# State-space layers unrolled, with the next layer's weight split and row normalisation beside the last chunk, decay sums of the first chunk ahead of the others, and the fourth stage's bias added tile by tile

## What is computed

```python
def _mamba2(u, in_w, conv_w, conv_b, dt_bias, A_log, Dp, rms_w, out_w):
    zxbcdt = u @ in_w.T                       # z, x, B, C, dt
    dt = softplus(dt + dt_bias)
    xBC = silu(causal_conv4(xBC) + conv_b)
    state = exp(dt * A) * state + (dt * x) B^T;  y = C . state + D * x
    y = y * silu(z)
    y = y * rsqrt(mean(y * y) + EPS) * rms_w
    return y @ out_w.T
h = x
for i in range(2):                            # N_LAYERS
    res = h
    h = layernorm(h) * ln_w[i] + ln_b[i]
    h = _mamba2(h, ...) + res
# fourth stage: t = t + (scan(...) * silu(z)) @ out_proj_w.T + out_proj_b
```

## Time and profile before

| | us |
|---|---|
| median of 3 runs | 1520.24 (1516.73 to 1520.94) |
| the profiled execution | 1520.59 |
| its span | 1518.6 |
| first layer opens, up to the first chunk's first exp | 100 to 171.7 |
| first layer's chunks | 171.7 to 380.8 |
| between the layers, up to the next first exp | 380.8 to 454.6 |
| second layer's chunks | 454.6 to 662.2 |
| end of the stage | 662.2 to 680.3 |
| fourth stage's opening | 744 to 788 |

### The profile page before, as it was taken

How to read it: one execution, slowest core, us unless ns; L and a number is a source line. 1 busy time by engine, 2 the same in 40 slices (tenths; PEclk the granted TensorE clock), 3 DMA queues, 4 the chain that set the end, 5 groups by cost and what they waited for, 6 DMA issues and landing times.

```text
span 1518.6 us, 33907 instructions
## 1 busy us (share of the span) xinstructions
PE 1245.3 (82%) x12366; PEld 857.0 (56%) x12367; DVE 1019.9 (67%) x1683; ACT 777.6 (51%) x1276; POOL 284.4 (19%) x350
## 2 busy tenths in 40 slices
PE   4724699998368999856569999787999999999996
PEld 2204576764256776623235555364776777777674
DVE  3667688887658888867766667566656674566432
ACT  3228567675567677722443433353546664475331
POOL 0111133333302333221120000005111111111111
PEclk9756799999679999977869999857999999999998
DMA  4034000001210000023220000046635663446111
GB/s 143 1 117 152 11 7 6 5 4 61 89 37 6 7 3 4 5 69 153 71 117 18 0 0 0 28 151 202 222 115 183 220 242 105 164 142 239 21 28 21
DMA packets 37799, 120.32 MB, mean 79 GB/s; under 512 B 9624, under 2 KB 13656, under 8 KB 27744
## 3 DMA queue, kind: packets, MB, share of 16 engines
q1 hardware_dynamic: 32080, 107.28, 19.7%
...
## 4 chain that ended last, share of the span: by engine, by line
PE 65%; DVE 13%; ACT 9%; issue 5%; DMA 3%; POOL 2%; DVEq 0%; POOLq 0%; ACTq 0%; SPq 0%
PE banks L2177 15%; PE banks L2156 14%; PE banks L996 10%; PE banks L1687 6%; PE banks L1717 3%; ACT mb_ca L824 2%; PE banks L1106 2%; PE banks L1067 1%; DVE mb_ca L622 1%; PE banks L1020 1%; PE banks L1057 1%; PE banks L2126 1%; PE banks L339 1%; DVE sq L259 1%; ACT mb_E L874 1%
## 5 line engine op out<-in xcount | busy, mean ns | idle before, releaser
L2156 PE MATMUL banks<-eb_x_hi,eb_w_hi 128*128 128x128 f16 x1344 | 227.6, 220 | 4.6 <-DVE eb_w_lo L2036 4.6
L2156 PE MATMUL banks<-eb_x_lo,eb_w_hi 128*128 128x128 f16 x1344 | 227.6, 220 | 0.0
L2156 PE MATMUL banks<-eb_x_hi,eb_w_lo 128*128 128x128 f16 x1344 | 227.5, 220 | 0.0
L996 PE MATMUL banks<-mb_u_hi,mb_wi_hi 128*128 (+3 forms) x1088 | 190.9, 222 | 13.8 <-ACT mb_ca L824 13.8
L996 PE MATMUL banks<-mb_u_hi,mb_wi_lo 128*128 (+3 forms) x1088 | 190.7, 221 | 0.0
L996 PE MATMUL banks<-mb_u_lo,mb_wi_hi 128*128 (+3 forms) x1088 | 190.5, 221 | 0.0
L2036 DVE TENSOR_TENSOR eb_w_lo<-eb_raw,eb_w_hi 128x2048 f32 (+1 forms) x64 | 142.6, 2287 | 23.0 <-ACT eb_w_hi L2042 16.0
L622 DVE SCALAR_TENSOR_TENSOR mb_ca<-mb_xp,mb_par,mb_ca 128x128 f32<-128x128 f32 x384 | 145.3, 440 | 5.9 <-ACT mb_ca L824 3.9
L2156 PEld LDWEIGHTS banks<-eb_x_hi,eb_w_hi 128*128 128x128 f16 x1344 | 132.0, 98 | 7.4 <-issue 5.0
L2156 PEld LDWEIGHTS banks<-eb_x_lo,eb_w_hi 128*128 128x128 f16 x1344 | 132.0, 98 | 2.4
L2156 PEld LDWEIGHTS banks<-eb_x_hi,eb_w_lo 128*128 128x128 f16 x1344 | 132.0, 98 | 0.0
...
## 6 DMA issues: line engine op xcount, KB each, us to landing
...
```

What stands on the lines that cost most here:

```text
L996: x = e.matmul(ps[0:width, bank, n * P:(n + 1) * P], a[:, k, f:f + width], b[:, k, ds(i * P, P)], start=(k == 0 and m == 0), stop=(k == KD ...
L2156: o = e.matmul(ps[:, j, c * P:(c + 1) * P], a[:, side, k, f * P:(f + 1) * P], b[:, k, :], start=(k == 0 and m == 0), stop=(k == KD - 1 and ...
```

## The change

- All engines: the layer loop is written out (`for l in range(LAYERS)`). The loop over the six middle chunks stays.
- `layer_open`, `ring_free` and ACT's square roots are gone; POOL takes the power -0.5 of the variance (`root`), over 128x8.
- `uf` is laid out by feature block. ACT evacuates 128x512 at a time, half of the tokens (four tiles) after the other, and writes the fp16 half of the even blocks itself; POOL's casts are gone. In the second layer PE projects the first chunk's x as soon as the first half is split.
- The next layer's pieces: `upper` 0 and 1 and `lower` 0 and 1 stand inside the last chunk, 2 and 3 just behind it. Their loads and the next parameters are issued in the last chunk.
- At the layer's end the sum of squares stands ahead of the output projection (eight matmuls in place of POOL's three adds and one matmul); seven tiles are aggregated and five normalised before the last tile is added.
- The first chunk's sum is made, split and sent ahead of the others (`first_sums`, `split_sums`). The split of the other seven tiles (now from SBUF, `sums`) and `lower(l, 5)` move on DVE into the first chunk, between the eighth `M` and `conv`; `upper(l, 5)` stands on ACT ahead of the silu; `dend` and `edec` behind z's silu.
- End of the stage: the residual is read back into `wi_hi` once z of the last chunk is made, and seven tiles are added and measured (`whole`) in and behind the last chunk; `row_stats` is gone in the second layer.
- Fourth stage: the bias is added per tile, after that chunk's y.

The core of the diff:

The buffer for the residual.

```diff
+    back = wi_hi[:].rearrange("p k f -> p (k f)").bitcast(F32)[:, 0:TT * D].rearrange("p (i f) -> p i f", i=TT)
```

```diff
+        def piece(l, n):
+            m = l * MB_PIECES + n
+            if m >= 2:
+                e.wait_ge(w_hi, m - 1)
+                e.wait_ge(w_lo, m - 1)
+            if n < KD:
+                e.dma_start(raw[n % 2], W_IN[l, n * P:(n + 1) * P, :]).then_inc(raw_in[n % 2], 16)
+            else:
+                e.dma_start(raw[n % 2][:, 0:4 * D].rearrange("p (j f) -> p j f", j=4),
+                            W_OUT[l, (n - KD) * 512:(n - KD + 1) * 512, :].rearrange("(j p) f -> p j f", p=P))\
+                    .then_inc(raw_in[n % 2], 16)
...
+            e.dma_start(cum_rows[:, 0:P], cum[0:MB_CR, 0:P]).then_inc(cum_out, 16)
...
+            e.wait_ge(prep, 2 * l + 2)
+            e.dma_start(cum_rows[:, P:TOK], cum[0:MB_CR, P:TOK]).then_inc(cum_out, 16)
...
+            if l + 1 < LAYERS:
+                for n in range(KD):
+                    piece(l + 1, n)
+                e.wait_ge(dx_done, (l + 1) * TT)
+                e.dma_start(par[:], ins["m_par"][l + 1, :, :]).then_inc(par_in, 16)
...
+        e.wait_ge(z_mm, 2 * LAYERS * TT)
+        e.dma_start(back, kept).then_inc(t_back, 16)
```

```diff
+            for half in range(2):
+                for k in range(KD):
+                    split_u(l, half, k)
+                if l == 0:
+                    lower(0, 2 + half)
...
+            def split_sums(source, columns):
+
+                rest = sums[:, columns]
+                own(e.tensor_tensor(rest[0:MB_CR, :], source, cum[0:MB_CR, columns], ALU.subtract))
+                e.tensor_copy(cum[H2:2 * H2, columns], rest[H2:2 * H2, :])
+                own(e.tensor_copy(cum[2 * H2:MB_CR, columns], rest[2 * H2:MB_CR, :]))
+                e.tensor_tensor(cum[2 * H2:MB_CR, columns], rest[2 * H2:MB_CR, :], cum[2 * H2:MB_CR, columns], ALU.subtract)\
+                    .then_inc(prep, 1)
...
+            e.wait_ge(first_ev, l + 1)
+            split_sums(ps[0:MB_CR, 6, 0:P], slice(0, P))
...
+                    if k == 4 and is_first:
+                        e.wait_ge(sums_exp, l + 1)
+                        own(e.tensor_tensor(dte[:], dend[:], dt[:], ALU.mult))
...
+                if is_first:
+                    e.wait_ge(sums_ev, l + 1)
+                    later = slice(P, TOK)
+                    own(e.tensor_copy(cum[0:MB_CR, later], sums[0:MB_CR, later]))
+                    split_sums(sums[0:MB_CR, later], later)
+                    lower(l, 5)
+                if is_last and l + 1 < LAYERS:
+                    lower(l + 1, 0)
+                    lower(l + 1, 1)
+                if is_last and l + 1 == LAYERS:
+                    e.wait_ge(t_back, 16)
+                    whole((0, 1, 2))
...
+                    if l + 1 < LAYERS and not is_first:
...
+                    if is_last and l + 1 == LAYERS:
+                        whole((3,))
...
+            def whole(tiles):
+
+                for i in tiles:
+                    own(e.tensor_tensor(t[:, i, :], h[:, i, :], back[:, i, :], ALU.add))
+                    e.bn_stats(core.stats[:, i, :], t[:, i, :])
...
+            if l + 1 < LAYERS:
+                e.wait_ge(stats_done, TT - 1)
+                aggregate(0, TT - 1)
+                lower(l + 1, 2)
+                row_norm(last)
+                lower(l + 1, 3)
+                e.wait_ge(rstd_done, 3)
+                e.wait_ge(ysq_done, last + 1)
+                normalise(range(5))
+                add_rows(TT - 1, last)
+                row_stats(TT - 1, last)
+                e.wait_ge(stats_done, TT)
+                aggregate(TT - 1, TT)
+                normalise((5, 6))
+                e.wait_ge(rstd_done, 4)
+                normalise((7,))
+            else:
+                row_norm(last)
+                whole((4, 5, 6))
+                own(e.tensor_tensor(h[:, TT - 1, :], h[:, TT - 1, :], back[:, TT - 1, :], ALU.add))
+                add_rows(TT - 1, last)
+                e.wait_ge(h_done, last + 1)
+                e.bn_stats(core.stats[:, TT - 1, :], t[:, TT - 1, :])
 
     OWN_PER_CONV = 2 * (TAPS - 2)
...
+            for half in range(2):
```

```diff
+                    e.activation(uf[:, k, columns], ps[:, TURNED_TO[half][k], :], ACT.Identity, scale=scale, bias=bias)\
+                        .then_inc(uf_done, 1)
+                    if k % 2 == 0:
+                        e.activation(u_hi[:, k, columns], ps[:, TURNED_TO[half][k], :], ACT.Identity, scale=scale, bias=bias)\
+                            .then_inc(uhi_done, 1)
+                if l == 0:
+                    upper(0, 2 + half)
...
+            if l:
+                e.wait_ge(halo, l * TT)
+                e.wait_ge(xc_done, 2 * l * TT)
+                evacuate_x(l * TT, 0)
             e.wait_ge(dtn_done, l + 1)
             own(e.activation(dte_[:], dtn[:], ACT.Exp))
             e.activation(dte_[:], dte_[:], ACT.Ln, bias=1.0).then_inc(dt_log, 1)
+            if l:
+                evacuate_x(l * TT, 1)
+                evacuate_bc(l * TT, True)
+                first_sums()
+            else:
+                evacuate_x(0, 0)
+                first_sums()
+                evacuate_x(0, 1)
+                evacuate_bc(0, True)
+            e.wait_ge(sums_mm, l + 1)
+            e.activation(sums[0:MB_CR, P:TOK], ps[0:MB_CR, 4:6, :].rearrange("p b n -> p (b n)")[:, P:TOK], ACT.Copy)\
+                .then_inc(sums_ev, 1)
             upper(l, 5)
-
-            def decay_sums():
...
+            own(e.activation(dend[:], ps[:, 7, 0:TT * H2].rearrange("p (i h) -> p i h", i=TT), ACT.Exp))
...
+                if is_last and l + 1 < LAYERS:
+                    e.wait_ge(z_mm, 2 * (l + 1) * TT)
+                    upper(l + 1, 0)
+                    upper(l + 1, 1)
...
+            if l + 1 < LAYERS:
+                upper(l + 1, 2)
...
+            if l + 1 < LAYERS:
+                upper(l + 1, 3)
```

```diff
+            e.wait_ge(w_lo, l * MB_PIECES + KD)
+            if l:
+                e.wait_ge(ulo_done, l * 2 * KD + KD)
+                project_x(0, 0)
+                project_x(0, 1)
+            e.wait_ge(ulo_done, (l + 1) * 2 * KD)
+            project_dt()
+            if l:
+                project_x(0, 2)
+                project_x(0, 3)
+                project_bc(0, l * TT)
+            else:
...
+            sum_tile(6, 0, first_mm)
...
+            e.wait_ge(ysq_done, (l + 1) * TT)
+            for j in range(JD):
+                x = e.matmul(ps[:, 2, 384:385], ysq[:, j, :], core.ones[:, 0:1], start=(j == 0), stop=(j == JD - 1))
+            x.then_inc(rms_mm, 1)
```

```diff
+            e.wait_ge(bias_added, g + 1)
...
-        e.tensor_tensor(t[:], t[:], outb[:].unsqueeze(1).to_broadcast([P, TT, D]), ALU.add).then_inc(bias_added, 1)
+
+        def body(i, first, last):
+            e.wait_ge(y_done, i + 1)
+            core.apart(e)
+            e.tensor_tensor(t[:, i, :], t[:, i, :], outb[:], ALU.add).then_inc(bias_added, 1)
+
+        chunks(e, body)
```

369 lines of the change are left out of this document (166 added, 203 removed).

## The result

| | before | changed |
|---|---|---|
| median | 1520.0 us (1516.7 to 1520.9, 4 runs) | 1481.6 us (1478.6 to 1482.3, 4 runs) |
| ratio | | 0.9747, 95% interval 0.9727 to 0.9767 |
| profiled execution, span | 1520.6, 1518.6 | 1482.3, 1480.5 |
| granted clock, mean | 0.896 | 0.909 |
| instructions | 33907 | 33584 |

38.4 us less, where 34 were forecast. A later set of five executions of the changed kernel gave 1482.4 and the ratio 0.9746 (0.9726 to 0.9767).

What follows compares the result with a forecast made beforehand. Prediction: the time to win lies where no engine is busy, mainly the engine-by-engine chain between the layers. First layer 9.3 - 8.0, between layers 28.4 - 8.0, end 4.9, fourth stage 7.3: 33.9 off 1520.59, median 1486, range 1475 to 1499 us.

Steps and rivals of the forecast that it cites:

- What the first chunk pays: Each layer's first chunk: DVE's moved split and lower half cost 6.65, the clock after PE's pause 1.3; loss 8.0 us (5 to 11).
- Between the layers: Second layer's opening, from last chunk to first exp: four steps together gain 28.4 us.
- normalised rows: Between the layers: rows normalised at 394.9 instead of 400.7, gain 5.8 us (4 to 7), the 2.76 fetch stall among it.
- halves: Between the layers, normalised rows to split input: no piece waited for, 6.7 instead of 19.5 us; gain 12.8 (11 to 14).
- first exp: Between the layers, from `la` to the first exp: 16.0 instead of 21.6 us; gain 5.6 (3 to 8), ACT's order the bound.
- First layer's opening: First layer up to its first exp: 162.4 instead of 171.74, gain 9.3 us (6 to 12).
- End of the stage: After the second layer: earlier residual read-back and additions beside the output product end it at 674.9, not 680.25; gain 4.9 (3 to 6).
- Fourth stage: Third lower half no longer waits for POOL's long bias addition: dt starts 7.5 earlier, eight short additions cost 0.2; gain 7.3.
- A: Rival: PE stays at half clock after pauses, or the first chunks cost the upper end; 12 given back, 1498 us; 14%.
- B: Rival: no clock loss, no wait for the eight matmuls, first chunk's PE pause overlaps; gain 41, 1479 us; 12%.
- C: Rival: fourth stage gains nothing, its eight additions on the path or lower 3 slow otherwise; 1494 to 1496 us; 7%.
- D: Rival: written-out layer code stalls 2.76 us at each stretch's first run; with 14 stalls on the path 1525 us; 4%.

Runs made afterwards that it cites:

- both_moved: Changed kernel with DVE's split of the other seven tiles moved ahead of the first chunk and the last lower half spread between its Ms: 1467.4 us.
- upper_behind: Changed kernel with the upper half of the last output piece moved, on ACT, behind the silu of C: 1481.2 us.
- opening_acts: Changed kernel with ACT's last upper half behind the silu of C and the five decay exps behind the first chunk's second exp: 1478.3 us.
- opening_table: Changed kernel with ACT's last upper half and decay exps moved later, and one column of silu ahead of its wait for the convolution: 1478.2 us.
- squares_end: Changed kernel with the second layer's last squares summed by POOL's three additions and one matmul instead of eight fp32 matmuls: 1481.0 us.
- loop_out: Kernel before with the loop over the two layers written out on all five engines and no operation moved: 1516.8 us, ratio 0.9985.
- bias_only: Kernel before with only the fourth stage's bias added tile by tile behind each y: 1510.6 us, ratio 0.9949.

## Why the forecast was right, and where its steps were off

The forecast held: 1486 with 1475 to 1499, measured 1481.6, and the main mechanism with both prices. Part of its closeness is luck: in the parts that the change touches, 3.0 us too little for the first layer's opening stand against 1.8 too much for the end, 0.7 in the second layer's last chunk and 0.5 between the layers. Runs of their own show the fourth stage's term, the loop's 2.9, what the first chunks pay and what the eight matmuls cost at the end. No run takes apart the rest of the openings' gains, the larger part of the whole (the split moved into the last chunk, the evacuations by halves, the first tile's sum ahead of the others); they are read from the timelines alone. Step by step:

**What the first chunk pays.** 8.0 a layer forecast, 8.2 and 7.8 measured. The convolution starts 7.4 behind the last `M` in both layers (6.7 forecast; the parts that the forecast lists add to 7.0), as the last lower half takes 3.31 beside POOL's convolution instead of 2.74; y comes 5.9 and 5.0 later, and the clock behind PE's 6.4 us of pause costs 2.3 and 2.8 instead of 1.3. both_moved shows that nothing else is in it. What the forecast missed is that the price was avoidable: 4.5 us of idle DVE stand ahead of the chunk.

**Between the layers.** 28.4 forecast, 27.9 measured, but the steps moved against each other:
- normalised rows: gain 3.3 instead of 5.8. The eight fp32 matmuls with one column take 3.57, no less than the row with 128 columns; I took 1.2 of its 3.0. This is the mis-sized term. The product behind them takes 7.4 at a granted clock of 0.72 instead of the 6.65 of the earlier trace rows.
- halves: from rows to split 7.5 instead of 6.7, gain 12.0 instead of 12.8. ACT's evacuations with scale and bias from the parameters start 0.66 apart, where I had 0.5. The Trainium skill (ScalarE: Activation LUTs, "What ACT_TABLE_LOAD costs") says that each operand given as one value per partition adds some 93 ns; by its figures the estimate for 512 columns and two such operands is 0.80, and the trace has 0.77 to 0.84.
- `la`: 7.8 instead of 8.6. PE was at full clock again after the first half of x.
- first exp: 14.0 instead of 16.0. The sums and the two products took 2.9 at a granted clock of 1.00, where I had given them 4.9, from the 3.04 of the earlier trace rows, which had run at 0.59.

**First layer's opening.** 12.3 instead of 9.3, the largest miss. Counted from A, lower 3 ends 0.7 earlier (1.6 forecast), from there to `la` it takes 7.7 instead of 12.8 (5.1 less, 5 forecast), and from `la` to the exp 15.05 instead of 21.6: 6.5 less. The failed step is the deduction "against it ACT now does upper 5, table, silu, z and two exps in a row", with which I went from about 12 to 9.3. ACT's upper half lies inside the time of DVE's convolution: upper_behind took it out of the row and gained nothing but 0.3 there. The sentence "ACT's order is the bound: upper 5 stands in front of the silu" falls with it, in both layers. In the first layer ACT's second silu waits for the convolution (0.49), and z, the table and the decay exps behind it reach to the exp; opening_acts takes the exps out of it, and from the evacuation to the exp it is 1.1 shorter than upper_behind. In the second layer the changed kernel has the same row behind the same wait (1.21), but there opening_acts gives only 0.2, since the table behind the wait and the upper half then make a row as long; opening_table takes 1.1 more.

POOL's power over eight columns took 1.69 and 1.65, not the 0.55 of one column; the second was on the path with 1.0 (the normalised rows start 9.6 behind A instead of 8.6), inside the bounds of -0.2 to 2.

**End of the stage.** 3.1 and -0.7 instead of 4.9. The failed term is the 1.2 for the eight matmuls again, which the product's end at 674.0 holds: they cost 3.15, by squares_end. The row additions beside it, 0.3 to 0.7 forecast for y, cost 0.7 at most, and that is not resolved: y1 to y7 differs by more between two kernels that have the same code there, 155.67 in the kernel before and 157.2 in loop_out.

**Fourth stage.** 7.3 forecast, 7.4 measured, 7.0 alone in bias_only. loop_out, with the fourth stage of the kernel before, takes 1.0 more than that kernel over the same distance, so the closeness of these three figures says little beyond 1 us; that the lower half takes 2.61 instead of 10.23 is what holds.

**The rivals.** A: the clock did fall at every place that it named (0.72 in the output product, 0.63 in x between the layers, 0.50 behind the pause), but the sums ran at full clock, and its 12 us are not there. B's full clock without a wait for the matmuls is not there either; the time lies between the forecast and B's 1479 because the opening was mis-sized and because of the 3.5 below. C and D are out by bias_only and loop_out.

**What the sum does not hold.** The gains in parts that the change touches add to 34.6 us, the forecast to 33.9. The other 3.5 of the 38.1 lie in the fourth stage's end and the last stage. The fourth stage's end has two values in these profiles: 14.2 in ten and 15.7 to 15.9 in four, the kernel before among them. By stretch, the kernel before:

```profile
964.90:981.60 16.70, 10.04 (x32) 4.50 (x32) 5.66 (x16) 1.02 (x1) 0.00 (x0) 0.69 0.00 1
```

The changed kernel:

```profile
930.10:945.20 15.10, 8.47 (x32) 4.01 (x32) 5.65 (x16) 1.02 (x1) 1.29 (x1) 0.77 0.00 1
```

loop_out, whose fourth stage is that of the kernel before:

```profile
964.20:978.40 14.20, 8.48 (x32) 3.60 (x32) 4.81 (x7) 1.02 (x1) 0.00 (x0) 0.76 0.00 0
```

The stretches hold the same 24 matmuls of the last product, at a mean granted clock of 0.69, 0.77 and 0.76. So in the profiled executions these 3.5 are not the change's. The medians differ by 38 too, twice; whether a part of those parts' difference is the rule in unprofiled executions, these runs don't settle.
